# Attention scores from three bfloat16 parts, one head per product, in place of two fp32r parts with two heads side by side

## The reference, cut to what matters

```python
q = (x @ Wq.T + bq).reshape(B, T, 16, 16).transpose(0, 2, 1, 3)    # the same for k and v
logits = jnp.einsum('bhqd,bhkd->bhqk', q, k) / jnp.sqrt(16.)
logits = jnp.where(causal, -jnp.inf, logits)
attn = jax.nn.softmax(logits, axis=-1)
out = jnp.einsum('bhqk,bhkd->bhqd', attn, v)
```

## Time and profile before

| | us |
|---|---|
| median of 3 runs | 3034.74 (3022.49 to 3039.16) |
| profiled execution: its own time | 3024.25 |
| profiled execution: span of its instructions | 3022.5 |
| first block: projections, main part | 545 to 745 |
| first block: heads, first score product to last copy | 763.05 to 1239 |
| second block: projections, main part | 2112 to 2184 |
| second block: heads | 2201 to 2681 |

### The profile page before, as it was taken

One profiled execution on the slowest core, in us unless ns is written; L12 is line 12 of the kernel. 1 busy time (PEld: TensorE's weight loads), 2 busy tenths in 40 slices (PEclk: granted clock), 3 DMA queues, 4 the chain that ended last, 5 costly groups with the idle time before them and its releaser, 6 DMA issues. The chain is left out here.

```text
span 3022.5 us, 48833 instructions
## 1 busy us (share of the span) xinstructions
PE 2505.5 (83%) x15234; PEld 1765.1 (58%) x15250; DVE 1935.7 (64%) x5450; ACT 1381.2 (46%) x2926; POOL 1041.4 (34%) x1430
## 2 busy tenths in 40 slices
PE   7966995787899999659939994996879999975998
PEld 6846993554444444348728983774744444434776
DVE  7754885563788788248737874773568888823544
ACT  4423552232277677314415552333627667741433
POOL 5774444664011111216764446650201111110000
PEclk9987997898599899769969996998959888976999
DMA  4444554565455444433445544331745545334010
GB/s 138 164 145 132 179 180 139 174 211 155 60 81 86 72 73 64 116 127 139 156 122 165 179 162 137 112 96 58 260 61 85 77 70 82 62 111 140 22 35 28
DMA packets 240443, 351.77 MB, mean 116 GB/s; under 512 B 36193, under 2 KB 169874, under 8 KB 240194
## 3 DMA queue, kind: packets, MB, share of 16 engines
q1 hardware_dynamic: 200258, 239.55, 33.2%
q0 software_dynamic: 39936, 109.11, 10.5%
HBM read 188.94 MB, written 157.81 MB: 115 GB/s over the span
## 5 line engine op out<-in xcount | busy, mean ns | idle before, releaser
L979 DVE CUSTOM_DVE_ANT_0 attn_heads_unused<-attn_heads_s_ps,attn_heads_causal 128x1024 bf16<-128x1024 f32 (+7 forms) x1024 | 719.2, 754 | 183.7 <-PE attn_heads_s_ps L864 182.9
L945 ACT ACTIVATE attn_heads_probs<-attn_heads_st_ps 128x512 f32<-128x512 f32 x1152 | 611.9, 600 | 339.2 <-PE attn_heads_st_ps L885 335.9
L864 PE MATMUL attn_heads_s_ps<-attn_heads_k_st,attn_heads_q_st 48*128 48x512 f32 (+3 forms) x1536 | 449.9, 422 | 81.8 <-DVE attn_heads_row_max L979 40.4
L831 POOL TENSOR_SCALAR_AFFINE_SELECT attn_heads_probs<-attn_heads_probs 128x512 f32<-128x512 f32 x256 | 157.7, 638 | 819.6 <-ACT attn_heads_probs L945 819.6
L885 PE MATMUL attn_heads_st_ps<-attn_heads_q_st,attn_heads_k_st 50*128 50x512 f32 (+3 forms) x1536 | 423.5, 415 | 3.0 <-ACT attn_heads_probs L945 2.8
L885 PEld LDWEIGHTS attn_heads_st_ps<-attn_heads_q_st,attn_heads_k_st 50*128 50x128 f32 x1536 | 240.9, 206 | 249.6 <-ACT attn_heads_probs L945 173.5
L864 PEld LDWEIGHTS attn_heads_s_ps<-attn_heads_k_st,attn_heads_q_st 48*128 48x128 f32 x1536 | 270.5, 216 | 160.1 <-DVE attn_heads_row_max L979 102.2
L902 PE MATMUL attn_heads_o_ps<-attn_heads_probs,attn_v_sb 128*32 128x512 f32 (+3 forms) x3072 | 355.0, 553 | 0.6 <-POOL attn_heads_probs L831 0.6
L1450 POOL DMA_INDIRECT xs_dram<-moe_route_xn,rows_at x256 | 272.5, 1064 | 79.0 <-issue 76.4
L1945 POOL DMA_DIRECT2D ys_dram<-moe_expert_y_sb x288 | 157.6, 547 | 243.8 <-DVE moe_expert_y_sb L2063 243.8
L2019 ACT ACTIVATE moe_expert_xT_hi<-moe_expert_xT_ps 128x256 fp32r<-128x256 f32 x288 | 110.7, 384 | 194.5 <-PE moe_expert_xT_ps L1963 193.8
(11 more groups left out here) (260 smaller groups left out, 5845.3 us busy)
## 6 DMA issues: line engine op xcount, KB each, us to landing
moe_expert_x_sb<-xs_dram SPq DMA_DIRECT2D x288, 128.0 KB, 2.1
ys_dram<-moe_expert_y_sb POOLq DMA_DIRECT2D x288, 128.0 KB, 2.1
attn_heads_q_st<-q_dram SPq DMA_DIRECT2D x192, 128.0 KB, 6.7
attn_heads_k_st<-k_dram SPq DMA_DIRECT2D x192, 128.0 KB, 7.2
q_dram<-attn_proj_parts SPq DMA_DIRECT2D x32, 512.0 KB, 3.5
k_dram<-attn_proj_parts SPq DMA_DIRECT2D x32, 512.0 KB, 5.2
o_dram<-attn_heads_oT SPq DMA_DIRECT2D x64, 256.0 KB, 2.9
moe_route_w_raw<-in_L_ffn_we_dram SPq DMA_DIRECT2D x96, 128.0 KB
```

The costliest lines, as they stand in the source:

```text
L831: last = pool.affine_select(out=d, in_=d, compare_op=ALU.is_ge, fill=0.0, base=0, pattern=[[0, QUAD], [1, P]], channel_multiplier=-1)
L864: made = pe.matmul(s_ps[:, use % SB, to:to + w], q_st[low:low + DEPTH, r, h // 2, i * P:(i + 1) * P], k_st[low:low + DEPTH, r, h // 2, a:a ...
L945: act.activation(to, from_, ACT.Exp, scale=scale).then_inc(exp_done, 1)
L979: last = dve.tensor_tensor_reduce(out=unused[:, scratch % 4, 0:w], in0=s_ps[:, use % SB, at:at + w], in1=causal[:, SEQ - w:SEQ], scale=1.0 ...
```

## The change

The projections write three bfloat16 parts of q and k. The first part is ACT's copy, the remainder goes to `rest` (DVE), the second part is ACT's copy of it (`second`), and the third is again a remainder (DVE, `third`). PE's next product into the same bank waits for `rest_ready` instead of `parts_ready`. The turned copies `x_hi` and `x_lo` of the next tile lie between these in the second block, and `find_moments` comes after `third(t, 2)`.

In the heads, q and k are bfloat16 and all heads start at partition 0. Six products of parts are stacked to 96 rows, and three rows hold the maxima (99 rows). Scores go to a ring of 4 single banks, a unit (one head, one tile of queries) taking one or two of them and freed by itself. There are 12 steps and 48 pieces per quad in place of 10 and 36. The maxima are split on POOL before they are turned (`split_max`, four small instructions), so PE turns them with a bfloat16 matmul, DVE makes one copy and SP writes three rows in one transfer. POOL sets the rows of -1 itself.

```diff
-        parts = sb("parts", [P, RP, PARTS, TILE], F32R)
+        parts = sb("parts", [P, 2, 4, SPLIT, TILE], BF16)
+        rest = sb("rest", [P, 2, TILE])
...
                     if t:
-                        pe.wait_ge(parts_ready, (t - 1) * 4 + m + 1)
+                        pe.wait_ge(rest_ready, (t - 1) * 4 + m + 1)
...
+                def second(t, m):
+                    act.wait_ge(rest_ready, 4 * t + m + 1)
+                    act.activation(parts[:, t % 2, m, 1, :], rest[:, m % 2, :], ACT.Copy).then_inc(second_ready, 1)
...
-                    for m in range(4):
-                        first(t, m)
-                        if not combine and 1 <= m <= KD and t + 1 < TILES:
-                            x_hi(t + 1, m - 1)
+                    first(t, 0)
+                    first(t, 1)
+                    second(t, 0)
+                    if not combine and t + 1 < TILES:
+                        x_hi(t + 1, 0)
+                    first(t, 2)
+                    second(t, 1)
+                    if not combine and t + 1 < TILES:
+                        x_hi(t + 1, 1)
+                    first(t, 3)
+                    second(t, 2)
+                    second(t, 3)
...
+                def third(t, m):
+                    dve.wait_ge(second_ready, 4 * t + m + 1)
+                    dve.tensor_tensor(parts[:, t % 2, m, 2, :], rest[:, m % 2, :], parts[:, t % 2, m, 1, :], ALU.subtract)\
+                       .then_inc(parts_ready, 1)
...
+QUERY_ORDER = (5, 4, 1, 2, 7, 6, 0, 3)
+LEAD = 9
+TURN_AFTER = 2
-STEPS = [(0, (0,)), (0, (1, 3)), (0, (2,)), (1, (0,)), (1, (1,)), (1, (2,)), (1, (3,)), (1, (4,)), (1, (5, 7)), (1, (6,))]
+STEPS = [(half, j) for half in range(2) for j in range((half + 1) * SUB)]
...
+PACE = (0, 0, 1, 2, 4, 4, 4, 5, 5, 7, 7, 7, 8, 9, 10, 11, 11, 11, 12, 13, 14, 15, 15, 16, 16, 17, 17, 18, 20, 20, 21,
+        21, 23, 24, 24, 25, 25, 26, 27, 28, 28, 28, 28, 28, 29, 29, 31, 32)
+COPY_AFTER = (9, 28)
+VALUES_AFTER = {2: -3, 5: -2, 8: -1, 12: 0, 18: 1, 22: 2, 25: 3, 31: 4, 35: 5, 38: 6, 41: 7, 44: 8}
...
-    DEPTH = 3 * HD
-    ROWS = DEPTH + PARTS
+    DEPTH = 6 * HD
+    ROWS = DEPTH + SPLIT
...
+                    for at, (ql, kl) in enumerate(((0, 0), (1, 0), (2, 0), (0, 1), (1, 1), (0, 2))):
+                        to = slice(at * HD, (at + 1) * HD)
+                        sp.dma_start(q_st[to, r, :, :], q_v[ql]).then_inc(stack_loaded[r], 16)
+                        sp.dma_start(k_st[to, r, :, :], k_v[kl]).then_inc(stack_loaded[r], 16)
...
+                def split_max(m):
+                    p = m % 2
+                    part = [max_parts[:, p, l * UNITS:(l + 1) * UNITS] for l in range(SPLIT)]
+                    pool.wait_ge(s_free, quad_over(m))
+                    if m >= 2:
+                        pool.wait_ge(s_free, turn_over(m - 2))
+                    pool.tensor_copy(part[0], row_max[:, p, :]).then_inc(part_step, 1)
+                    pool.wait_ge(part_step, 3 * m + 1)
+                    pool.tensor_tensor(max_rest[:, p, :], row_max[:, p, :], part[0], ALU.subtract).then_inc(part_step, 1)
+                    pool.wait_ge(part_step, 3 * m + 2)
+                    pool.tensor_copy(part[1], max_rest[:, p, :]).then_inc(part_step, 1)
+                    pool.wait_ge(part_step, 3 * m + 3)
+                    pool.tensor_tensor(part[2], max_rest[:, p, :], part[1], ALU.subtract).then_inc(parts_ready, 1)
...
+                for n in range(NQ):
                     for s in DIAGONAL:
+                        if s == SUB * 2 and n + 1 < NQ:
+                            split_max(n + 1)
                         mask(n, s)
...
+                    for a in range(0, (i + 1) * P, TILE):
+                        w = min(TILE, (i + 1) * P - a)
+                        last = pe.matmul(s_ps[:, at + a // TILE, 0:w], q_st[0:DEPTH, r, h, i * P:(i + 1) * P],
+                                         k_st[0:DEPTH, r, h, a:a + w], start=True, stop=True)
+                    last.then_inc(s_full, 1)
...
+                    pe.matmul(st_ps[:, v % NB, 0:w], k_st[0:ROWS, n % R, h, j * P:(j + 1) * P],
+                              q_st[0:ROWS, n % R, h, first:first + w], start=True, stop=True).then_inc(st_full, 1)
...
-    q_dram = dram("q_dram", [BATCH, PARTS, D, SEQ])
+    q_dram = dram("q_dram", [BATCH, SPLIT, D, SEQ], BF16)
```

More of the change, by code:

```diff
@@ L42 @@
 SPLIT = 3
-PARTS = 2
 LOWEST = -3e38
@@ L570, in _ @@
                 for t in range(TILES):
+                    take_first(t, 0)
+                    take_first(t, 1)
+                    third(t, 0)
+                    if not combine and t + 1 < TILES:
+                        x_lo(t + 1, 0)
+                    take_first(t, 2)
+                    third(t, 1)
+                    if not combine and t + 1 < TILES:
+                        x_lo(t + 1, 1)
+                    take_first(t, 3)
+                    third(t, 2)
                     if not combine and t + 2 < TILES:
                         find_moments(t + 2)
-                    for m in range(4):
-                        take_first(t, m)
-                        if not combine and 1 <= m <= KD and t + 1 < TILES:
-                            x_lo(t + 1, m - 1)
+                    third(t, 3)
                     if not combine:
@@ new lines, with score_banks, place @@
+VALUES_AFTER = {2: -3, 5: -2, 8: -1, 12: 0, 18: 1, 22: 2, 25: 3, 31: 4, 35: 5, 38: 6, 41: 7, 44: 8}
+def score_banks(quads, banks):
+    last = [0] * banks
+    units, turns = [], []
+    at = use = 0
+    def place(width):
+        nonlocal at, use
+        if at + width > banks:
+            at = 0
+        spot = (at, use, max(last[at:at + width]))
+        use += 1
+        last[at:at + width] = [use] * width
+        at = (at + width) % banks
+        return spot
+    for g in range(quads * QUAD * QT):
+        k = g % (QUAD * QT)
+        units.append(place(-(-(QUERY_ORDER[k % QT] + 1) // SUB)))
+        if k == TURN_AFTER and g > k:
+            turns.append(place(1))
+    turns.append(place(1))
+    return units, turns
@@ L693, in heads_phase @@
[L693 to L694 removed]
     NB = 3
     NR = 4
[L697 to L700 removed]
+    DEPTH = 6 * HD
+    ROWS = DEPTH + SPLIT
     LOAD = 12 * 16
[L702 to L705 removed]
+    SB, OB = 4, 1
+    UNIT_AT, TURN_AT = score_banks(NQ, SB)
@@ new lines, in turn_max, with scores_t @@
+                def turn_max(m):
+                    at, _, over = TURN_AT[m]
+                    pe.wait_ge(parts_ready, m + 1)
+                    pe.wait_ge(s_free, over)
+                    pe.matmul(s_ps[0:SPLIT * UNITS, at, 0:P], max_parts[:, m % 2, :], identb[:, :],
+                              start=True, stop=True).then_inc(s_full, 1)
+                def scores_t(n, s, h):
+                    half, j = STEPS[s]
+                    first, w = step_queries(half, j)
+                    v = n * PIECES + s * QUAD + h
@@ L879, in scores_t @@
                     if v >= NB:
                         pe.wait_ge(exp_done, v - NB + 1)
-                    low = (heads[0] % 2) * GROUP
-                    for x, h in enumerate(heads):
-                        for j, first, w, at in step_columns(s):
-                            to = x * step_width(s) + at
-                            last = pe.matmul(st_ps[:, v % NB, to:to + w], k_st[low:low + ROWS, n % R, h // 2, j * P:(j + 1) * P],
-                                             q_st[low:low + ROWS, n % R, h // 2, first:first + w], start=True, stop=True)
@@ new lines, in _ @@
+                for g in range(NQ * UNITS):
+                    n, k = divmod(g, UNITS)
+                    h, i = k // QT, QUERY_ORDER[k % QT]
+                    (at, use, _), w = UNIT_AT[g], (i + 1) * P
+                    if k == 0 and n >= 2:
+                        dve.wait_ge(parts_ready, n - 1)
+                    dve.wait_ge(s_full, use + 1)
+                    dve.tensor_tensor_reduce(out=masked_s[:, use % 4, 0:w], in0=s_banks[:, at * TILE:at * TILE + w], in1=causal[:, SEQ - w:SEQ],
+                                             scale=1.0, scalar=LOWEST, op0=ALU.add, op1=ALU.max,
+                                             accum_out=row_max[:, n % 2, h * QT + i:h * QT + i + 1]).then_inc(s_free, 1)
+                    if k == TURN_AFTER and n > 0:
+                        copy_turn(n - 1)
```

320 lines of the change are left out of this document (106 added, 214 removed).

## The result

The kernel after takes 3004.93 us (median of 6 runs, 2998.01 to 3005.26) against 3033.59 us for the kernel before (6 runs beside it, 3022.49 to 3042.44): a ratio of 0.9905, 95% interval 0.988 to 0.993. It is faster by about 1%, where I forecast 1% slower. In a later set of runs on another chip the ratio was 0.9922 (0.9895 to 0.9949). Its profiled execution took 3004.83 us, 19.4 us less in span than the one of before; the medians lie 28.7 us apart. The kernel before spreads over 20 us from run to run and the one after over 7, and only the first has stretches of low clock in its quads.

The account below looks back on a forecast made before the run. PE and DVE, nearly equal and waiting on each other, were taken to bound the heads. Heads +14 and projections +17 made +31 us on the profiled 3024.25, 3055; against the median 3034.74, 3066 us, range 3010 to 3135.

Parts of the forecast that it names:

- What bounds the kernel, and PE's own work: Heads: PE and DVE nearly equal before, waiting on each other; PE's own work after 26.6 us a quad (24.9 to 27.8).
- waits shrink: 0 at best, 3.6 as now at worst, taken 1.2: Heads: DVE and ACT 4 to 6 us below PE, so PE's waits a quad fall from 3.6 to 1.2 us.
- The 3.6 for before: Heads: in the kernel before, PE and DVE waiting on each other were put at 3.6 of a 26.1 us quad.
- The clock: Heads: low-clock stretches cost 1.2 us a quad before; taken as 0.3 (0 to 1.5) after.
- values steps and waits on ACT still break the stream: Heads: argument against the rival of a high clock and queues never dry; no size of its own.
- The turn: Heads: turning the maxima moves to POOL, 0.3 us of PE stall a quad (0 to 1.5); 0.2 in the sum.
- The first quads: Start of each heads phase: the first quad falls from 34.0 to 29 us as the clock rises sooner, -5.
- and behind them stand x_hi, x_lo and normalise that PE waits for. Between 0 and 2.4 us a tile; taken 1.0: Second projection: ACT and DVE hand products back and forth twice, delaying work PE needs; 1.0 us a tile, +8.
- Faster: Rival: heads' clock stays high and queues never run dry; quad 26.4 us, projections covered (+5), -35, 3000 us; chance 0.15.

Follow-up runs that it names:

- h3: The kernel after with two buffers in place of three for the transposed scores; 3344.17 us beside 3139.7 for the kernel before.
- the zero rows: The kernel before with rows of zeros padding the half-height score matmuls to 62 and 64 rows; 2986.14 us, ratio 0.9869, and 0.9839 with zeroing by buffer.
- p4: The kernel before with only find_moments(t + 2) moved from the start of a tile to before its fourth take_first; 3022.88 us, ratio 1.000.
- after_again: The kernel after, unchanged, run again on another chip; 3004.18 us, ratio 0.9922 to the kernel before.
- p1: The kernel after with find_moments(t + 2) back at the start of a tile; 2978.22 us, ratio 0.9847 to the kernel before.
- b2: The kernel before with scores contracted over all 128 rows in float32r, without pairs (other sums computed); 3309.48 us beside 3139.7 for the kernel before.
- b3: The kernel before with 14 rows of zeros per head, so half-height scores contract over 62 and 64 rows; 2986.14 us, ratio 0.9869.
- b4: The kernel before with the same rows of zeros, set buffer by buffer; 3112.94 us beside 3154.66 for the kernel before, ratio 0.9839.
- b1: The kernel before with all score matmuls on rows 0 to 49, so no pairs (other sums computed); 3919.57 us beside 3139.7 for the kernel before.
- h2: The kernel after with three of six products, scores contracted over 48 (51) rows in place of 96 (99), unpaired; 3701.63 us, one run.

## Why the prediction was wrong

**What bounds the kernel, and PE's own work: right.** I had PE at 26.6 us a quad, 16.0 for the scores, 9.3 for the values and 1.3 for entering them. A quad is 26.66 us, all of it PE. Summed over 13 quads of the trace the terms are 16.2, 9.4 and 1.1. The narrow matmuls are not held up by their loads (128 columns start 0.06 us apart), but the 512-column ones start 0.218 and 0.225 us apart in the mean, not 0.215; a 512-column values step takes 0.998; and entering the values costs 0.09 us (0.309 from a last 512-column score to the first value, for 0.218), not 0.12. The stated upper bound of 27.8 doesn't come out of its terms, which add up to 27.1.

**The step that failed: "waits shrink: 0 at best, 3.6 as now at worst, taken 1.2".** They are 0.03 us a quad. This was a mis-sized term in a right mechanism: DVE at 22.5 and ACT at 21.4 us are 4 to 5 us below PE, and with the buffers that this kernel has, engines so far ahead don't delay the one that sets the pace. The buffers belong to it: with two for the transposed scores (h3) the gaps in work are the same and PE stands still for 3.5 us a quad. 1.2 x 28 = 34 us of the error. The 3.6 for before was itself too much: it is 26.1 less a PE of 22.5 that has every matmul in a pair, while the view has PE standing still for 1.6 us of that quad.

**The clock: right sign, too small.** I named 1.2 us a quad before and took 0.3 for after. After has 0 in the full quads: 0.3 x 28 = 8 us. The 1.2 itself was good; the zero rows lift exactly this (27.3 to 26.0, 1.3 us). But I treated the low clock as a remainder of broken rhythm. It hangs on the rows at work: at equal instructions, 96 rows 1.00 and 48 rows 0.50; in pairs, 48 and 50 rows 0.92, 62 and 64 rows 0.99 to 1.00; with 10% of PE's time lost in short waits and 96 or 99 rows still 1.00. How many rows are enough isn't measured: only these points are. My counter-argument under the rival, "values steps and waits on ACT still break the stream", was refuted: values steps stay and the clock is 1.00, in h3 with waits on ACT too. The Trainium skill (TensorE: Matmul & The Clock Gate, What's actually happening) ties the clock to how busy PE has been. A PE busy for 640.3 of 640.6 us at clock 0.50 shows that busy in the trace's sense doesn't suffice; the measurement decides.

**The turn, 0.2 us a quad: 0.** (The text derives 0.3; its sum uses 0.2.) No wait of PE on `parts_ready` shows. With the waits and the clock, 1.7 x 28 = 48 of the 55 us by which the heads were missed (forecast +14, measured -41). The first quads give most of the rest: they were 6 and 8 us shorter than before, not 5. The quads of the second heads were 27.5 us before and 26.6 after.

**The second projection: the step "and behind them stand x_hi, x_lo and normalise that PE waits for. Between 0 and 2.4 us a tile; taken 1.0".** Measured 4.0 in the steady tiles, outside the range. I added up work by engine and gave the moved `find_moments` no line at all. It closes a ring from one tile's remainders over moments, POOL, xn and the turn to the next tile's products: 9.6 us without the added work (p4), 13.3 with it, against a tile of 9.3. Its price has two parts: 2.19 us of a still PE, and products at 0.43 for 0.23 us behind it. In the first projection the same additions cost 2.3 us in these two traces, not 6; other traces of the two orders have this stage at 267.6 (p4) and 270.3 (after_again), so its price is small and not settled. The gathers cover most of it: DVE's waits for gathered rows fell from 25.5 us to 8.1.

**The rival that came true** is "Faster": quad 26.4 (26.66 measured), 3000 us (3004.93 measured), by its named mechanism, with the projections at +25 where it had +5 and the heads at -41 where it had -40. I gave it 0.15 for want of trust in an engine with no waits. That its time came within 5 us is partly luck. Its quad had 26.1 us of PE and 0.3 of waits, where 26.6 and 0.03 were measured; the traces differ by only 19 us where it had 35; and the rest comes from the other stages and from the run of before that was profiled, 9 us under its median. 3004.93 also lies below the range.

**Was the change needed?** Against a kernel before whose clock is held (26.0 us), the change costs 0.65 us a quad: its own work and its vanished waits together are a small loss, and the net gain in the full quads is the clock that it holds with its 96 rows. The two best kernels stand level: p1 at 0.985 of before, the zero rows at 0.984 to 0.987.

## What to carry to other kernels

Price a low clock as a term that an edit can remove, and ask what in the array holds it down: with half-height tiles, try padding with rows of zeros before anything else. When one engine has 4 us more work than the others and three or more buffers lie between them, try a wait of zero in the sum; with two (h3), or with scores freed two banks at a time (b2), it wasn't zero. And when an edit both adds work to in-order engines and moves a producer later, neither price alone says anything: follow the ring from that producer round to itself and compare its length with the period.

## What the hardware showed that was not expected

- Rows of zeros raise the granted clock: 48 and 50 rows to 62 and 64 in each half, 0.92 to 1.00 in the first heads (b3); 0.99 on another chip (b4).
- A lone half height of 48 to 51 rows runs at 0.50 in spite of a PE almost without a pause, in bfloat16 (49.7 us a quad) and float32r (53.3).
- At that clock a half-height 512-column bfloat16 matmul takes 0.43 us, its columns at 1.2 GHz and nothing more. The 0.12 us over the columns that I read from the half-height float32r ones isn't there; in float32r at the same clock two take 1.02 us (b1, 1002.73 to 1003.75), and at full height and a clock of 1.00 some start 0.33 us apart (b2). So in these runs it goes with float32r, not with few rows.
- At a clock of 0.99 to 1.00 a float32r weight load takes 187 to 188 ns, with 62, 64 or 128 rows (b4, b2), a bfloat16 one 97 to 98 with 96 and 99 rows. At 0.50 they take longer, 319 (b1) and 129 (h2). Why some float32r matmuls of 512 columns start 0.23 us apart and others 0.33 stays open.
